# Two edits in a fused scan and feed-forward kernel: the centre tap of the convolution moves from GpSimd to VectorE, and the row of scales is kept in bf16

## The reference

```python
# layer 0, attention part
u = einsum('btd,nd->btn', x, W_in)
sel_h = silu(einsum('btd,hd->bth', x, W_sel_in))
a, b, c, dg = sigmoid, tanh, tanh, sigmoid of the four parts of sel_h @ W_sel_out.T
h_t = a_t * h_{t-1} + b_t * u_t
y = c * h + d_param * dg * u
return einsum('btn,dn->btd', y, W_out)
# feed-forward part (D_MODEL 1024, D_HIDDEN 4096)
h = bit_linear(x, w1)                  # act_quant per token, weight_quant per tensor
h = depthwise_conv1d(h, conv_w, conv_b)   # 3 taps, padding 1
h = silu(h)
return bit_linear(h, w2)
# both layers
x = x + _layernorm(_L0_attn_ref(_layernorm(x), ...))
x = x + _layernorm(_L0_ffn_ref(_layernorm(x), ...))
# act_quant: scale = 127 / max|x| of the token; round(x * scale) / scale
```

## Time and profile before

| | |
|---|---|
| median of 2 runs | 3504.55 us (3502.76 to 3506.34) |
| the profiled execution | 3503.06 us |
| span of its slowest core (core 2) | 3501.4 us |
| spans of the eight cores | 3472.3 to 3501.4 us |
| granted TensorE clock, mean, core 2 | 0.766 |
| busy: TensorE matmuls | 1663.4 us (48%) |
| busy: VectorE | 1420.5 us (41%) |
| busy: ScalarE | 1227.0 us (35%) |
| busy: GpSimd | 892.6 us (25%) |
| read from and written to HBM | 232.85 MB, 25.17 MB |

### The profile page before, as it was taken

The page is one execution under the profiler, slowest core; times in us unless marked ns, Lnnn a source line. Parts: engine busy times, 40 slices in busy tenths (PEclk is TensorE's granted clock), DMA queues, the critical chain, the costliest instruction groups (busy, mean ns, idle before and its releaser), DMA issues.

```text
span 3501.4 us, 35569 instructions; the slowest of 8 cores (3472.3 to 3501.4 us)
## 1 busy us (share of the span) xinstructions
PE 1663.4 (48%) x8464; PEld 878.0 (25%) x8464; DVE 1420.5 (41%) x4092; ACT 1227.0 (35%) x1961; POOL 892.6 (25%) x1393
## 2 busy tenths in 40 slices
PE   0000015365556564656464656565655565655553
PEld 0000014041414141414141414141423132323130
DVE  1120224444444444444444443535353536353342
ACT  1343333333333333333333333434343434332121
POOL 0000002322222323232323232323232323232222
PEclk9999987576868686868687768776768677877775
DMA  5555710303030303031313121212121212121303
GB/s 181 174 173 175 212 63 1 93 22 98 23 94 27 93 29 93 28 89 32 90 32 87 34 82 39 81 40 79 43 76 45 74 47 60 49 67 42 81 28 97
DMA packets 112700, 260.34 MB, mean 74 GB/s; under 512 B 12656, under 2 KB 12656, under 8 KB 112496
## 3 DMA queue, kind: packets, MB, share of 16 engines
q1 hardware_dynamic: 97808, 212.97, 20.9%
q0 software_dynamic: 10080, 36.70, 3.6%
q10 hardware_dynamic: 4608, 8.39, 0.6%
HBM read 232.85 MB, written 25.17 MB: 74 GB/s over the span
## 4 chain that ended last, share of the span: by engine, by line
DMA 23%; PE 16%; DVE 16%; POOL 13%; ACT 12%; issue 10%; DVEq 6%; ACTq 2%; POOLq 2%; SPq 0%
DMA w2sb<-w2s 13%; POOL h L828 8%; DVEq L57 6%; PE pD L994 5%; DVE h L838 4%; DMA stgF<-w1T 4%; PE pE L994 4%; DVE h L846 4%; PE pE L799 3%; DMA stgF<-w2T 2%; DMA w2s<-stgb 2%; POOL h L978 2%; POOLq L57 2%; POOL stgF L1053 2%; ACT hpre L808 2%
## 5 line engine op out<-in xcount | busy, mean ns | idle before, releaser
L799 PE MATMUL pE<-xqw,w1t 128*128 128x258 bf16 x4352 | 596.3, 302 | 194.7 <-ACT hpre L808 191.0
L994 PE MATMUL pD<-w2sb,h 128*128 128x512 bf16 x1024 | 429.9, 513 | 502.9 <-DMA w2sb<-w2s 365.5
L799 PEld LDWEIGHTS pE<-xqw,w1t 128*128 128x128 bf16 x4352 | 463.9, 108 | 323.1 <-issue 219.8
L828 POOL TENSOR_SCALAR h<-hpre,cwt,cbt 128x256 bf16<-128x256 bf16 x544 | 332.5, 623 | 629.4 <-ACT hpre L808 629.4
L994 PE MATMUL pE<-w2sb,h 128*128 128x512 bf16 x1024 | 444.1, 528 | 42.7 <-DMA w2sb<-w2s 28.8
L978 POOL TENSOR_SCALAR h<-k2i,onec,rccn 128x512 bf16<-128x512 int32 x272 | 266.6, 980 | 529.7 <-ACT k2i L974 483.1
L838 DVE SCALAR_TENSOR_TENSOR h<-hpre,cwt,h 128x256 bf16<-128x256 bf16 x544 | 227.5, 480 | 427.1 <-POOL h L828 427.1
L808 ACT ACTIVATE hpre<-pE 128x258 bf16<-128x258 f32 x544 | 184.3, 386 | 612.4 <-DVE h L846 526.3
L974 ACT ACTIVATE k2i<-k2f,rcc 128x512 int32<-128x512 bf16 x272 | 196.3, 722 | 385.5 <-DVE k2f L963 274.2
L994 PEld LDWEIGHTS pD<-w2sb,h 128*128 128x128 bf16 x1024 | 74.4, 103 | 850.3 <-issue 849.9
L754 DVE COPY xqw<-xqw 128x8 bf16<-128x8 bf16 x16 | 3.0, 186 | 696.0 <-ACT xqw L747 696.0
(11 more groups left out here) (177 smaller groups left out, 2122.4 us busy)
## 6 DMA issues: line engine op xcount, KB each, us to landing
w2sb<-w2s SPq DMA_DIRECT2D x544, 256.0 KB, 2.7
xin<-x SPq DMA_DIRECT2D x16, 1024.0 KB, 5.6
stgF<-w1T POOLq DMA_DIRECT2D x32, 512.0 KB, 4.1
stgF<-w1T SPq DMA_DIRECT2D x32, 512.0 KB, 4.6
stgF<-w2T POOLq DMA_DIRECT2D x32, 512.0 KB, 4.2
stgF<-w2T SPq DMA_DIRECT2D x32, 512.0 KB, 4.6
out<-stgF SPq DMA_DIRECT2D x32, 512.0 KB, 2.9
w2s<-stgb ACTq DMA_DIRECT2D x16, 256.0 KB, 4.1
```

The source lines that it names most:

```text
L799: lambda e, S, c=c, k=k, off=off, pf=pf: e.matmul(pE[:, off:off + 258], w1t[:, 4096 * k + 128 * c:4096 * k + 128 * (c + 1)], xqv[:, pf, k, :],
L828: e.tensor_scalar(hd, hs[:, 1:257], cwt[:, 3 * cc + 1:3 * cc + 2], cbt[:, cc:cc + 1], OP.mult, OP.add),
L994: coff=coff: e.matmul(bank[:, 512 * jj:512 * (jj + 1)], h4[:, 256 * c + 128 * s:256 * c + 128 * (s + 1)], w2sb[:, coff:coff + 512], start= ...
```

## The change

Two edits. The centre tap and bias of each group of four chunks, four tensor_scalar, are made by VectorE and not by GpSimd. VectorE then waits for ScalarE's copy (`A_evh`) itself, and, at a window's first group, for the last W2 matmul of the window before (`PE_w2`); its wait for GpSimd is gone. And `bc2` is bf16 in place of float32, so that L940 casts, and both inputs of L963 are bf16. Everything behind L828 has a line number that is 4 lower.

```diff
-        bc2 = sb("bc2", [128, 256], F32)
+        bc2 = sb("bc2", [128, 256], BF16)
...
-                    q.wait("g", "ac", A_evh[f][c])
+                    q.wait("v", "ac", A_evh[f][c])
                     if c == 3 and f > 0:
-                        q.wait("g", "pe", PE_w2[f - 1])
-                    g_t2 = 0
+                        q.wait("v", "pe", PE_w2[f - 1])
                     for cc in range(c - 3, c + 1):
                         hs = hpre[:, 258 * (cc % 5):258 * (cc % 5 + 1)]
                         hd = h4[:, 256 * cc:256 * (cc + 1)]
-                        g_t2 = q.op("g", lambda e, S, cc=cc, hs=hs, hd=hd:
-                                    e.tensor_scalar(
-                                        hd, hs[:, 1:257], cwt[:, 3 * cc + 1:3 * cc + 2],
-                                        cbt[:, cc:cc + 1], OP.mult, OP.add),
-                                    sem="gp")
-                    q.wait("v", "gp", g_t2)
+                        q.op("v", lambda e, S, cc=cc, hs=hs, hd=hd: e.tensor_scalar(
+                            hd, hs[:, 1:257], cwt[:, 3 * cc + 1:3 * cc + 2],
+                            cbt[:, cc:cc + 1], OP.mult, OP.add))
                     q.drain("v")
```

## The result

| | before | after |
|---|---|---|
| median of the runs | 3505.74 us (8 runs) | 3368.95 us (9 runs) |
| ratio | | 0.9611, 95% interval 0.9596 to 0.9627 |
| the profiled execution, its slowest core's span | 3503.06, 3501.4 us | 3364.56, 3363.0 us |

The kernel is 3.9% faster, 137 us by the medians, inside the range of 3280 to 3410 us. The forecast was 5.2%, 183 us: the direction and the mechanism hold, and a quarter of the gain is missing. That quarter is what the experiments are about. One of the nine runs after the change, of 3389.20 us, had a granted clock of 0.71 on four of its cores, and the ratio leaves it out.

What follows compares the result with a forecast made beforehand. No engine bounds the kernel but a chain of hand-offs, with DVE waiting for POOL in the convolution. Thirteen windows give 142 us, the first two 18, the last two 24: 183 off 3503.1, median 3321 us, range 3280 to 3410.

Steps and rivals of the forecast that it cites:

- POOL's leg: Convolution loop: POOL's four L828 operations and one hand-off, 2.44 + 0.16 us, leave it; new loop 6.11 us, 1.10 less.
- the clock did not fall: Rival, chance 3%: denser work lowers TensorE's granted clock, making the kernel slower than before, 3560 us.
- T0: End of a window's first group of four chunks (its last L846); forecast 4.3 us earlier.
- The first two windows: Windows with no pair of additions in POOL's way; forecast gain 9.0 us each, 18 us in all.
- Term 1: Convolution loop: tensor_scalar of 128x256 on DVE takes 0.28 us, four of them 0.85 us.
- The first rival: DVE pays L838's price for the convolution's tensor_scalar; loop 6.93 us, gain 99 us, time 3404 us; chance 20%.
- Term 2: Window start: on DVE the tensor_scalar no longer waits for POOL's two L1053 additions; T0 comes 4.3 us earlier.
- POOL's two additions hold DVE up: Rival at window start: the first group's tensor_scalar waits for POOL's L1053 additions; 14 us lost, 3335 us; chance 14%.
- T2: End of a window's third group of four chunks; forecast 4.1 to 5.8 us earlier, 4.9 taken.
- Term 3: Third group of a window: TensorE's matmuls behind attention's decide T2, 4.9 us earlier, the earlier groups' gains included.
- The second edit and its filling of the pipe: bc2 in bf16 shortens L963 and L978 where DVE, ACT and POOL fill the pipe; 1.5 us a window, bounds 0.6 and 2.3.
- The last two windows: Windows with no attention beside them; forecast gain 11.9 us each, 24 us in all, with T0 3.4 us sooner.

Runs made afterwards that it cites:

- the probe: Kernel before, with rows of bf16 DVE operations put ahead of its work, some beside seven POOL additions, results unused; 3568.03 us in a single run.
- the constants experiment: Changed kernel with constants 0.5 and 0.1 for the tensor_scalar's weight and bias columns; 3303.24 us in a single run, beside 3500.65 before.
- the run without additions: Changed kernel with POOL's two residual additions at a window's start cut from 1024 to 8 columns; 3350.08 us, ratio 0.9519.
- the quarters: Changed kernel with each of POOL's residual additions made in four pieces of 256 columns; 3371.02 us, ratio 0.9581.
- the tap on ScalarE: Changed kernel with centre tap and bias made by ScalarE from PSUM, DVE keeping the outer taps; 3302.43 us, ratio 0.9385.

## Why the prediction was right, and where its sizes were off

**Right.** POOL's leg left the loop; the max/min lost their cover and stand ahead of the tensor_scalar; ScalarE's copies still wait for the last tap; the W2 waits stayed (366.5 us in 403 waits, and 365.5 in 402 before); L959 fell to 0.29 us and L974 towards 0.8; the clock did not fall. Two of the signs that I named for it did not come, the tensor_scalar at 0.25 to 0.3 us and T0 some 4 us sooner; these are terms 1 and 2. The first two windows came out at 17.8 of 18 us. That agreement is chance in part: there was hardly a hold there (one addition before window 1, beside which the four took 1.35 us), but L826 cost more, so that bc2 came 6.5 us sooner in each and not 7.5, and what follows bc2 made up for it (2.1 and 2.7 us where I had 1.5).

**Term 1, the tensor_scalar at 0.28 us, 0.85 for four.** It took 0.343, and 1.12. The step that failed is "column operands cost 0.05". I had it from L838 (480 ns, with a column) against L892 (0.43 us, with a constant), so one column for 0.05, and then charged it once to an operation that has two. Two at 60 ns on the 222 of constants give 342. That stretches the loop by 0.27; another 0.07 are hand-offs, 0.15 instead of 0.08 ahead of L826. The first rival (L838's rate, 0.48 each) did not come: the rate is that of the fast operations (0.26 ns a column; 128x1024 with constants took 422 ns in the probe, L318 435).

At the rate of the constants experiment (3.5 us a window for 0.48 a group), 0.27 us is worth 2.0 us a window.

The rule of "Advanced Engine Details and Errata" of the Trainium skill, VectorE Performance Modes, on a start on 4 bytes is not borne out: 343 ns at either address. "Vector Engine (DVE) Microarchitecture Reference" of the Trainium skill, section 5.1, which says that it makes no difference, agrees with the runs.

**Term 2, T0 at 4.3 us sooner.** It came 1.6 sooner; of the 2.7 missing, 2.4 are the hold (the run without additions) and 0.3 the dearer operation. This is the rival "POOL's two additions hold DVE up", to which I gave 14% and which puts T0 at 15.2 us into the window (1793.7 less 1778.54), where 14.9 came. I had set it against the fact that POOL pays where L978 stands beside L963. Here POOL was first and DVE paid: each of the two held instructions started while an addition was under way and ended just behind it. I had looked for a gap before the tensor_scalar; there is none, the hold is in the instruction's own length. Its size was off as well. I priced it at 0.8 us a window, because I took T2 to be set by TensorE, and it is 1.6 by the profile, 1.9 by the ratios (the run without additions).

"SBUF — State Buffer", Who interferes with whom, of the Trainium skill has it that the one who comes first keeps the other out for its whole instruction. The trace agrees: 2.37 us beside additions of 2.34.

**Term 3, T2 set by TensorE, 4.9 us sooner.** That step failed: DVE sets it. My value is 25.6 us into the window (1804.2 by my middle, less 1778.54). Without the additions T2 is at 24.9 to 25.4 us in ten of windows 2 to 14, close to my bound for the quick TensorE (24.8), and at 26.5 to 26.9 in the other three, 25.4 in the mean. With them it is at 26.8 to 27.6, 27.0 in the mean, and DVE's row in the window of the table shows no wait for ScalarE there, the tensor_scalar 0.15 us behind the max/min:

```profile
1745.18 0.42 DVE L863 TENSOR_TENSOR accN<-accN,h 128x512 bf16<-128x512 bf16 x1
1745.75 1.12 DVE L826 TENSOR_SCALAR h<-hpre,cwt,cbt 128x256 bf16<-128x256 bf16 x4
```

So the forecast had given away to TensorE some of what terms 1 and 2 then took, and their 2.0 and 1.9 us do not add up in the table. The means of windows 2 to 14 give it by place: bc2 comes 2.45 us short of the forecast 9.4, of which 1.3 were lost up to T2 (4.9 forecast, 3.6 measured), where both terms and TensorE play together, and 1.2 behind T2 (4.5 forecast, 3.3 measured), where only the loop's 6.45 in place of 6.11 us is left. How the 1.3 divide between the hold and the dearer operation is open.

**The rest.** The second edit and its filling of the pipe: 8.3 less the 7.0 by which bc2 comes sooner leaves 1.3 us a window, where I had 1.5; bc2 alone, by its ratio, brought 1.1. The last two windows brought 16.2 of 24: T0 there was 22.7 us and is 21.3 in the last one, a gain of 1.4 and not 3.4, and seven loops at some 0.3 less each explain the remainder. The 3.1 us lost ahead of the first window lie in a stage that the change doesn't touch. The point scatters from core to core, too: from 555.67 to 562.26 us in the one trace before, from 555.60 to 560.80 in the one after. The 3.1 us are within that scatter, and the two slowest cores are different ones.

## What to carry to other kernels

When a step is moved to the engine that closes the loop, price it from rows with the same operands and count each column operand by itself: here two columns of 60 ns each on an operation of 222 made most of the difference between 6.1 and 6.4 us a loop. Ask also what the other engine is doing when the moved step starts, not only whether the new engine is free; an addition on GpSimd that is off the path can hold the step that is on it. And look for the engine that idles in the loop, even if it is slower at the operation: ScalarE's 565 ns beat VectorE's 343 by 2.3% of the run.

## What the runs showed of the hardware that I had not expected

- A column operand of tensor_scalar costs 60 ns, fixed (220, 281, 342 ns for none, one, two at 256 columns; 422 and 542 for none and two at 1024; two in bf16 take 342 as well).
- A float32 addition of 128x1024 on POOL holds not only a tensor_scalar (2.37 us in place of 0.34) but a scalar_tensor_tensor too (2.42 to 2.55 in place of 0.48), and is itself stretched from 2.34 to 2.52 us beside the latter.
- A held tensor_scalar ends 0.08 to 0.09 us behind the addition that was under way, be it 2.35 us long or a quarter of 0.73, and a held scalar_tensor_tensor 0.28 us behind it (read in one window each of the changed kernel, the quarters and the tap on ScalarE); the next addition then holds the next instruction. Cutting the addition into four shortens the longest hold from 2.39 to 0.92 us, but T0 gains 0.3 of 2.4 us: five instructions are held and not two.
